# Maxima transposed in bf16, second scores issued ahead of the copied maxima, retention scores in one step

## The reference

```python
x = _layernorm(x + _L0_attn_ref(x, ...))            # linear attention, MLP
x = _layernorm(x + _L0_xattn_ref(x, ctx_1024, ...)) # 16 heads, band of 64 tokens each way
x = _layernorm(x + _L0_ffn_ref(x, ...))             # 6 cells, each an attention of 8 heads
x = _layernorm(x + _L1_attn_ref(x, ...))            # retention: causal, no softmax
x = _layernorm(x + _L1_xattn_ref(x, ctx_1024, mask_BxS2_bk0, ...)) # 16 heads
x = _layernorm(x + _L1_ffn_ref(x, ...))             # product with a matrix made by Fourier
# an attention:  p = softmax(q @ k.T);  out = p @ v
# the retention: W = cumsum(k x v over tokens);  out = q @ W
```

## Time and profile before

| | |
|---|---|
| median of 3 runs | 3470.81 us (3463.22 to 3472.4) |
| profiled execution, its own time | 3470.35 us |
| its span, first to last instruction | 3468.6 us |
| PE busy | 3157.1 us, 91% |
| DVE, ACT, POOL busy | 67%, 49%, 35% |
| mean granted clock of TensorE | 0.967 |

### The profile page before, as it was taken

One profiled execution on the slowest core, in us unless ns is written; L12 is line 12 of the kernel. 1 busy time (PEld: TensorE's weight loads), 2 busy tenths in 40 slices (PEclk: granted clock), 3 DMA queues, 4 the chain that ended last, 5 costly groups with the idle time before them and its releaser, 6 DMA issues.

```text
span 3468.6 us, 77951 instructions
## 1 busy us (share of the span) xinstructions
PE 3157.1 (91%) x30860; PEld 2362.2 (68%) x30860; DVE 2319.2 (67%) x5004; ACT 1695.7 (49%) x3492; POOL 1202.3 (35%) x1308
## 2 busy tenths in 40 slices
PE   6889999999999999999999999999999999998866
PEld 5766666777676667667667776766777666666654
DVE  6676667667585776858677676867667585565533
ACT  1245464545546454454645545464544546454532
POOL 6886016162341606234160523416162341000000
PEclk8899999999999999999999999999999999999986
DMA  6211010010101001010100101010010101000000
GB/s 221 71 56 35 19 35 29 26 47 17 50 23 38 29 26 47 17 47 26 38 29 26 47 17 47 26 38 29 26 47 17 47 26 30 22 16 8 16 4 4
DMA packets 123283, 122.90 MB, mean 35 GB/s; under 512 B 9776, under 2 KB 122672, under 8 KB 122800
## 3 DMA queue, kind: packets, MB, share of 16 engines
q1 hardware_dynamic: 122928, 117.91, 11.2%
HBM read 113.69 MB, written 4.19 MB: 34 GB/s over the span
## 4 chain that ended last, share of the span: by engine, by line
PE 60%; DVE 16%; POOL 9%; issue 7%; ACT 6%; DMA 1%; SPq 1%; POOLq 0%; DVEq 0%; ACTq 0%
PE banks L750 17%; PE banks L742 13%; PE banks L888 7%; DVE nmx L1257 6%; PE banks L911 5%; PE banks L942 4%; POOL work L1648 4%; POOL work L1638 4%; ACT work L1488 3%; PE banks L1021 2%; PE banks L735 2%; PE banks L853 2%; DVE work L1218 2%; PE banks L898 1%; PE banks L949 1%
## 5 line engine op out<-in xcount | busy, mean ns | idle before, releaser
L750 PE MATMUL banks<-work,weights 128*128 128x256 f32 x3584 | 862.0, 388 | 19.4 <-DVE work L1281 13.5
L750 PEld LDWEIGHTS banks<-work,weights 128*128 128x128 f32 x3584 | 667.6, 192 | 161.3 <-issue 51.0
L1257 DVE TENSOR_REDUCE nmx<-banks 128x4 f32<-128x1024 f32 (+1 forms) x527 | 605.0, 1188 | 209.7 <-PE banks L888 209.3
L1488 ACT ACTIVATE work<-banks 128x1024 f32<-128x1024 f32 (+2 forms) x699 | 595.7, 913 | 281.5 <-PE banks L915 279.2
L742 PE MATMUL banks<-weights,work 128*128 128x256 f32 x2688 | 651.0, 388 | 29.9 <-DVE work L1281 12.3
L742 PEld LDWEIGHTS banks<-weights,work 128*128 128x128 f32 x2688 | 501.3, 193 | 132.9 <-issue 43.4
L1648 POOL TENSOR_TENSOR work<-work 128x512 f32<-128x512 f32 x256 | 400.1, 1582 | 202.2 <-DVE work L1218 105.1
L911 PE MATMUL banks<-work 32*128 32x256 f32 (+1 forms) x5120 | 395.2, 395 | 39.7 <-DVE nmx L1257 15.4
L888 PE MATMUL banks<-work 32*128 32x256 f32 (+1 forms) x5120 | 359.9, 396 | 67.1 <-ACT work L1390 37.6
L1638 POOL TENSOR_TENSOR work<-work 128x512 f32<-128x512 f32 x256 | 346.8, 1380 | 51.1 <-DVE work L1209 28.6
L1692 POOL TENSOR_TENSOR work<-work,row 128x512 f32<-128x512 f32 x64 | 107.6, 1681 | 731.0 <-PE banks L735 731.0
(11 more groups left out here) (160 smaller groups left out, 3753.2 us busy)
## 6 DMA issues: line engine op xcount, KB each, us to landing
weights<-in_w_all SPq DMA_DIRECT2D x322, 256.0 KB, 2.7
work<-in_w_setup SPq DMA_DIRECT2D x41, 256.0 KB, 5.8
work<-in_ctx SPq DMA_DIRECT2D x32, 256.0 KB, 3.0
work<-in_x SPq DMA_DIRECT2D x16, 256.0 KB, 2.9
out<-work SPq DMA_DIRECT2D x16, 256.0 KB, 2.2
weights<-in_w_all SPq DMA_DIRECT2D x1, 3072.0 KB, 12.8
row<-in_rows SPq DMA_DIRECT2D x1, 1280.0 KB, 9.2
mrow<-in_mask SPq DMA_DIRECT2D x16, 32.0 KB, 3.3
```

Of the source, the lines that this page charges most:

```text
L750: ins = e.matmul(b[:, m * 256:m * 256 + 256], wslot(w)[:, k, m * P:m * P + P], xin[:, k, :], start=(k == 0 and (m == 0 or closed)) if star ...
L1257: ins = e.tensor_reduce(nmax(s, n)[:, 2 * p + j:2 * p + end, :], b.rearrange("p j (c n) -> p j c n", c=NC)[:, :, :, 0:w], AX, ALU.max, neg ...
L1488: ins = e.activation(dst, b.rearrange("p j (c n) -> p j c n", c=NC)[:, :, :, 0:w], ACT.Exp)
```

## The change

Four things change in the code, and the order of all engines with them, since costs and seeds of the plan are new.

- `nm` multiplies the upper halves of `nmx`, read as bf16 (`nmax_parts`), with a bf16 identity, and ACT's copy writes bf16.
- `st` issues all products of the scores first, then waits for the copy, then adds the maxima: in kinds c and y with four matmuls of 512 columns in place of eight of 256. In the plan `st` needs the transposes (`b`), and `exp` needs the copy as well.
- `rs` is one step for each half f, with all four row groups; it takes five banks at once.
- the costs of `nm`, `st`, `rs`, of the maxima of kind x and of `band`, and `SEEDS`, are other numbers.

```diff
--- before.py
+++ after.py
@@ -70,7 +70,7 @@
 FIRST_ROWS = 3
 RSLOT = {n: i for i, n in enumerate(ROWS)}
 
-SEEDS = (271952, 450768, 66414, 843758, 204716)
+SEEDS = (66403, 758222, 122752)
 SLOTS = 10
 X, CT, XT = 0, 1, 2
 Z = 7
@@ -208,18 +208,18 @@
         kind, c, f, par = quad(n)
         b = do("PE", "s", n, 0.88, q, k, *((nm_done[n - 2],) if n >= 2 else ()),
                takes=("score", "score"))
-        maxed = [do("DVE", "s", (n, p), 1.13, b, frees=((b, p),)) for p in range(2)]
+        maxed = [do("DVE", "s", (n, p), 1.13 if kind != "x" else 1.21, b, frees=((b, p),)) for p in range(2)]
         maxed = [do("DVE", "split", n, 0.36, *maxed)]
-        b = do("PE", "nm", n, 0.22, *maxed, *((st_done[n - 2],) if n >= 2 else ()), takes=("misc",))
+        b = do("PE", "nm", n, 0.16, *maxed, *((st_done[n - 2],) if n >= 2 else ()), takes=("misc",))
         nm_done[n] = b
         nm = do("ACT", "nm", n, 0.28, b, frees=((b, 0),))
-        s = st_done[n] = do("PE", "st", n, 1.12 if kind != "x" else 1.0, nm, 
+        s = st_done[n] = do("PE", "st", n, 1.2 if kind != "x" else 1.08, b,
                             *(("PE", "fold", (k, c)) for k in "qkv" for c in (4, 5)), ("PE", "cb", 4), ("PE", "cb", 5),
                             takes=("score", "kept", "half"))
-        e = [do("ACT", "exp", (n, p), 0.91 if kind != "x" else 0.7, s, frees=((s, p),)) for p in range(2)]
+        e = [do("ACT", "exp", (n, p), 0.91 if kind != "x" else 0.7, s, nm, frees=((s, p),)) for p in range(2)]
         both = (do("DVE", "add", n, 1.2, *e),) if kind == "c" else ()
         if kind == "x":
-            e = [do("POOL", "band", (n, p), 1.0, e[p]) for p in range(2)]
+            e = [do("POOL", "band", (n, p), 1.22, e[p]) for p in range(2)]
         pv = do("PE", "pv", n, 1.3 if kind == "c" else 0.9, *e, *both, v,
                 frees=((s, 2),))
         if par == 0:
@@ -286,12 +286,10 @@
     state = through("r_state", 0, 0.85, "DVE", 0.4, scaled[1], ("PE", "r_q_t", 0))
     out = []
     for f in range(NC):
-        p0 = do("PE", "rs", (f, 0), 0.87, r_q_t, *((("PE", "rs", (f - 1, 0)),) if f else ()), takes=("half", "score", "ctx"))
-        m0 = do("DVE", "rs", (f, 0), 1.22, p0, frees=((p0, 1),))
-        p1 = do("PE", "rs", (f, 1), 0.87, p0, takes=("score",))
-        m1 = do("DVE", "rs", (f, 1), 1.22, p1, frees=((p1, 0),))
-        pv = do("PE", "rpv", f, 1.35, state, m0, m1, *((("PE", "rpv", f - 1),) if f else ()), frees=((p0, 0),))
-        out.append(do("ACT", "rpv", f, 0.36, pv, frees=((p0, 2),)))
+        p = do("PE", "rs", f, 0.95, r_q_t, *((("PE", "rs", f - 1),) if f else ()), takes=("half", "score", "score", "ctx"))
+        m = [do("DVE", "rs", (f, j), 1.22, p, frees=((p, 1 + j),)) for j in range(2)]
+        pv = do("PE", "rpv", f, 1.35, state, *m, *((("PE", "rpv", f - 1),) if f else ()), frees=((p, 0),))
+        out.append(do("ACT", "rpv", f, 0.36, pv, frees=((p, 3),)))
     r_o = through("r_o", 0, 0.44, "DVE", 0.66, *out)
     mb = do("ACT", "mb", 0, 0.9, ("PE", "rpv", 1))
     y_k = through("y_k_t", 0, 0.44, "DVE", 1.3, y_k, ("PE", "rpv", 1), also=(mb,))
@@ -642,15 +640,15 @@
 
             return small[s]["nmx"][:, n % 2].rearrange("p c (g r) -> p g c r", r=32)[:, :, :, part]
 
-        def upper(t):
-
-            return t.bitcast(BF16).rearrange("p (n h) -> p n h", h=2)[:, :, 1]
+        def nmax_parts(s, n, c):
+
+            return small[s]["nmx"].bitcast(BF16)[:, n % 2, c].rearrange("p (n h) -> p n h", h=2)[:, :, 1]
 
         def nmax_upper(s, n, part):
             return small[s]["nmx"].bitcast(BF16)[:, n % 2].rearrange("p c (g r h) -> p g c r h", r=32, h=2)[:, :, :, part, 1]
 
         def stored_nmax(s, n):
-            return slot(s, NMT[quad(n)[0]])[:, n % 2, :]
+            return slot(s, NMT[quad(n)[0]])[:, n % 2, :].bitcast(BF16)[:, 0:S]
 
         def queries(kind, kc):
             return slice(kc * WINDOW, kc * WINDOW + SPAN) if kind == "x" else slice(0, S)
@@ -895,27 +893,37 @@
                     e.wait_ge(*when("split", a, i))
                     b = take("misc", "nm", a, i)
                     for c in range(NC):
-                        ins = e.transpose(b[:, c * P:c * P + P], small[s]["nmx"][:, a % 2, c, :], ident[:, :])
+                        ins = e.matmul(b[:, c * P:c * P + P], nmax_parts(s, a, c), ident_bf[:, :], start=True, stop=True)
                     ins.then_inc(*tell(pe[s], "nm mm", a, i))
                 elif op == "st":
                     kind, c, f, par = quad(a)
                     q, k, v = operands(s, a)
                     b = [take("score", "exp", a, 0, i), take("score", "exp", a, 1, i)]
                     book(i, a)
-                    e.wait_ge(*when("nm", a, i))
-                    added_row = minus_bf if kind == "x" else ones_bf
                     for kc in range(NC):
                         qq = queries(kind, kc)
                         o = slice(kc * 256, kc * 256 + qq.stop - qq.start)
                         for g in range(4):
                             e.matmul(b[g // 2][g % 2][:, o], k[32 * g:32 * g + 32, f, kc * P:kc * P + P],
-                                     q[32 * g:32 * g + 32, f, qq], start=True, stop=False,
+                                     q[32 * g:32 * g + 32, f, qq], start=(kc == 0), stop=False,
                                      tile_position=(32 * g, 0))
+                    e.wait_ge(*when("nm", a, i))
+                    if kind == "x":
+                        for kc in range(NC):
+                            qq = queries(kind, kc)
+                            o = slice(kc * 256, kc * 256 + qq.stop - qq.start)
+                            for g in range(4):
+                                ins = e.matmul(b[g // 2][g % 2][:, o], minus_bf[32 * g:32 * g + 3, :],
+                                               stored_nmax(s, a)[32 * g:32 * g + 3, qq], start=False,
+                                               stop=(kc == NC - 1), tile_position=(32 * g, 0))
+                                if kc == NC - 1 and g == 1:
+                                    ins.then_inc(*tell(pe[s], "st mm", a, 0, i))
+                    if kind != "x":
                         for g in range(4):
-                            ins = e.matmul(b[g // 2][g % 2][:, o], added_row[32 * g:32 * g + 3, :],
-                                           upper(stored_nmax(s, a))[32 * g:32 * g + 3, qq], start=False,
-                                           stop=True, tile_position=(32 * g, 0))
-                            if kc == NC - 1 and g == 1:
+                            ins = e.matmul(b[g // 2][g % 2].rearrange("p (c n) -> p c n", c=NC), ones_bf[32 * g:32 * g + 3, :],
+                                           stored_nmax(s, a)[32 * g:32 * g + 3, :].unsqueeze(1).broadcast_to([3, NC, S]),
+                                           start=False, stop=True, tile_position=(32 * g, 0))
+                            if g == 1:
                                 ins.then_inc(*tell(pe[s], "st mm", a, 0, i))
                     ins.then_inc(*tell(pe[s], "st mm", a, 1, i))
                 elif op == "pv":
@@ -1006,23 +1014,21 @@
                                            stop=(par == 1))
                     ins.then_inc(*tell(pe[s], "r_state mm", i))
                 elif op == "rs":
-                    f, p = a
-                    if f == 0 and p == 0:
+                    if a == 0:
                         e.wait_ge(*when("r_q_t", i))
-                    if p == 0:
-                        book(i, f"r{f}")
-                    b = take("score", "rm", f, p, i)
-                    if p == 0:
-                        take("ctx", "rout", f, i)
+                    book(i, f"r{a}")
+                    b = [take("score", "rm", a, 0, i), take("score", "rm", a, 1, i)]
+                    take("ctx", "rout", a, i)
                     for par in range(2):
                         for c in range(NC):
-                            for j in range(2):
-                                g = 2 * p + j
-                                ins = e.matmul(b[j][:, par * S + c * P:par * S + c * P + P],
-                                               slot(s, XT)[32 * g:32 * g + 32, f, c * P:c * P + P],
-                                               slot(s, R_QT[par])[32 * g:32 * g + 32, f, c * P:c * P + P],
+                            for g in range(4):
+                                ins = e.matmul(b[g // 2][g % 2][:, par * S + c * P:par * S + c * P + P],
+                                               slot(s, XT)[32 * g:32 * g + 32, a, c * P:c * P + P],
+                                               slot(s, R_QT[par])[32 * g:32 * g + 32, a, c * P:c * P + P],
                                                start=True, stop=True, tile_position=(32 * g, 0))
-                    ins.then_inc(*tell(pe[s], "rs mm", f, p, i))
+                                if par == 1 and c == 1 and g == 1:
+                                    ins.then_inc(*tell(pe[s], "rs mm", a, 0, i))
```

(1 more changed line is left out.)

## The result

The changed kernel takes 3526.97 us (median of 4 runs, 3513.64 to 3531.9), the kernel before 3469.39 us beside it: a ratio of 1.0159, 95% interval 1.0135 to 1.0183. It is 57.6 us slower, where 55.5 us faster was forecast; no case that the prediction priced reaches this far, the slowest being 3485 us.

What follows compares the result with a forecast made beforehand. PE, 94% busy in the long middle, was taken as the bound. The terms -39.5 + 10 - 32 + 0 + 3 + 8 - 5 = -55.5 us took 3470.35 us to 3415 us, forecast 3395 to 3440 us, range 3370 to 3458 us.

Steps and rivals of the forecast that it cites:

- the slowest being 3485 us: Rival: PE's queue stands still at the joint retention step, 80 us of waits in place of 10; 3485 us, chance 0.10.
- What bounds the kernel: Whole kernel: between 400 and 3000 us PE is 94% busy, so almost any matmul time saved shortens the end.
- Retention: Retention scores: four row groups at once halve 79.0 us, a gain of 39.5 us; new waits of PE give back 10 us.
- Transposes: Transposes of maxima on PE: bf16 in place of float32 gains 32 us, bounds 0 and 70 us.
- The rival in which loads set the pace: Transposes of maxima: bf16 ones come no faster than their weight loads, so 32 us are not gained; 3447 us, chance 0.13.
- Second scores, with the wait: Second scores on PE: products and joint additions 0 us; waiting for ACT's copy before the additions +3 us, bounds 0 and 12.
- the order: Order of four entries on five engines: put at 0, with 40 us, a quarter of the middle's idle time, to either side.
- The 82 changes of the split of the array: PE changes its way of splitting the array 82 times more, 0.10 us each: +8 us, bounds 0 and 24 us.
- the -5 us at the end of the program: Last entry: some ten stages have ACT's copy now beside products, 0.5 us each: -5 us, bounds 0 and -10.
- The sign to look for: Profile after: PE busy falling by 60 us with a span that doesn't fall would make the order the cause.

Runs made afterwards that it cites:

- the better order: The changed kernel with only SEEDS replaced by three other random numbers (654503, 320699, 206964), so another order of steps: 3437.53 us, ratio 0.9903 to the kernel before.
- new_code_old_seeds: The changed kernel with the random numbers of the kernel before, so only the order of steps differs: 3697.58 us, ratio 1.0655 to the kernel before.

## Why the prediction was wrong

- *What bounds the kernel.* PE at 94% was read as a bound that any saving moves. It is a bound only with its order: the waits and the clock took up whatever the transposes freed in two orders of three, and 50 of the 70 us added in one.
- *Retention.* The forecast was -39.5 + 10 = -29.5 us. The gain in PE time was right, 41.5 us. The wait was over-sized: it is 19.4 us, 1.5 us longer than before, where +10 was put. The run that undoes the four groups gives 29.4 us, but that it equals the forecast is luck: it goes back to two rounds in one step, 20.3 us of cover, and not to the four steps of before. In another order it gives 7.9 us.
- *Transposes.* The size of PE time was right, 36.0 us against 32, with the two starts of a step 56 ns apart in the trace (the median). The end didn't move: -1.5 us in the order of before (a ratio of 0.9989), none in the new one. The rival in which loads set the pace is wrong: a load takes 100 ns, longer than the 56 ns between starts.
- *Second scores, with the wait.* +3 us were put for a wait between products and additions, which is 0.3 us; undone in the new order the edit shows 2.2 us the other way, and both are within the noise. In the better order the products ahead of the wait, with the joint additions, are worth 33 us, which the prediction put at nothing: it had seen that PE hardly waited for the copy, and that holds for the order of before alone.
- *The step that failed is the order.* The prediction said "the order of four entries on five engines is new, and no row prices that: I put 0, with 40 us [...] to either side". If four groups at once are worth 29 us in this order and the other edits nothing, it cost 57.6 + 29.4 = 87 us, an estimate, since edits were undone one at a time. The runs with exchanged numbers show what the bound should have been: 171 us for the changed code, 222 us for the code before. The 82 changes of the split of the array, 8 us, were all that the prediction's paragraph on the order counted. Their price was read between starts, not from the end of an addition as the prediction says, and no run measures it. Nor does a run measure the -5 us at the end of the program: after 3000 us PE is idle for 89.5 us, before 89.9.
- *The sign to look for.* "A PE busy time that falls by 60 us with a span that doesn't" would have named the order. PE busy fell by 28.4 us only, to 3128.7 where 3085 to 3110 was put, since unchanged groups took more.

Shown is that the order, not the code, lost the time: the edits of `nm` and `st` cost nothing in the order of before, no edit undone in the new order wins the time back, and the changed code in another order is faster than the kernel before. Shown too is that the loss is idle time of PE and PE time lost again in unchanged groups; that a lower clock is a part of the latter is an estimate. Not settled is which feature of the order does it. Uneven entries go with every slow order, and the five splits kept waiting beside POOL make 17.7 us of the idle time, but no run tests either alone. The joint retention step was never tried in the order of before.

## What to carry to other kernels

Where one list per engine fixes the order of several jobs, a change to the plan's costs or seeds is a change of its own: run the new code in the old order, and the old code in the new one, before crediting either. An engine that is busy for 94% can absorb a saving of 1% in waits and clock, so measure an edit in more than one order, one laid out for it among them. new_code_order_1, the changed code with other random numbers, beats both kernels: 3437.5 us, 1% under the kernel before. How much of that 1% is owed to the edits is open: its numbers were picked from many tries for the changed code, and no run gives the code before as many. In the two orders that nobody chose, the codes take the same time.

## What the runs showed of the hardware

- A two-input instruction of DVE on SBUF, eight elements for each partition, lasted 4.72 us beside four multiplications of POOL in a row and ended when POOL paused; the mean of its kind is 0.26 us. It does so at five places of the changed kernel (4.72 to 4.74 us), beside the same four multiplications, and at five of each of the three kernels with an edit undone in its order. The Trainium skill (SBUF — State Buffer, SBUF: two separate sides) calls the port pair that DVE and POOL share an exclusive lock, held for a whole instruction of the winner. By that the wait would be one multiplication, at most some 1.5 us here (an estimate from the 2.95 us of two); the trace shows one across several, and the measurement decides. That the pair is the cause is not tested by a run, and it does not rank the orders: in new_code_old_seeds, the slowest, no split lasts longer than 1.51 us.
- Sixteen row-group products of 128 columns take 37.5 / 32 = 1.2 us in four groups at once, where two rounds of two groups take 57.8 / 32 = 1.8 us.
- TensorE's mean granted clock moved with the edits in the order of before: over all executions 0.963 with PE time taken away and 0.972 with PE time added, against 0.965 and 0.964 for the kernel before beside them. There a saving on PE was in part paid back as lower clock. In the order of new_code_order_1 it was not so: with and without float32 transposes the clock is 0.969 and 0.968, at 38.4 us of PE time between them. With the order alone, the changed code's clock goes from 0.938 (new_code_old_seeds) to 0.968 (new_code_order_1).
